# Causal mask of the second row tile's scores: from identity products on TensorE to an add inside VectorE's row maximum

## The reference, cut to what matters

```python
scores = jnp.einsum('bhqd,bhkd->bhqk', q, k) / HEAD_DIM ** 0.5
causal = jnp.tril(jnp.ones((s, s), dtype=bool))
scores = jnp.where(causal[None, None], scores, -jnp.inf)
probs = jax.nn.softmax(scores, axis=-1)
out = jnp.einsum('bhqk,bhkd->bhqd', probs, v)
```

## Time and profile before

| | us |
|---|---|
| median of 3 runs (2930.70 to 2936.34) | 2931.71 |
| profiled execution, its own time | 2930.81 |
| span of that execution in the trace | 2929.1 |
| attention, steady part, 212.31 to 599.00 | 386.69 |

### The profile page before, as it was taken

How to read it: one execution, slowest core, us unless ns; L and a number is a source line. 1 busy time by engine, 2 the same in 40 slices (tenths; PEclk the granted TensorE clock), 3 DMA queues, 4 the chain that set the end, 5 groups by cost and what they waited for, 6 DMA issues and landing times.

```text
span 2929.1 us, 45881 instructions
## 1 busy us (share of the span) xinstructions
PE 2793.4 (95%) x16150; PEld 2283.9 (78%) x16150; DVE 1236.7 (42%) x2152; ACT 877.9 (30%) x1697; POOL 838.8 (29%) x1306
## 2 busy tenths in 40 slices
PE   6989999988999939999999999999999999999998
PEld 6865555556666529999999999999999999999997
DVE  6756777747888833332232232132133133133111
ACT  1126666641555512221121121122122122122110
POOL 4546776631166641101101111011021021011010
PEclk9999999999999969999999999999999999999999
DMA  3101222242122223221122032032033033022010
GB/s 109 43 1 31 48 45 48 55 92 87 68 84 75 77 83 106 91 86 64 51 92 75 26 108 83 15 109 87 12 108 101 11 100 104 14 90 85 26 47 21
DMA packets 97078, 194.68 MB, mean 66 GB/s; under 512 B 22126, under 2 KB 23758, under 8 KB 96800
## 3 DMA queue, kind: packets, MB, share of 16 engines
q1 hardware_dynamic: 75072, 131.77, 15.1%
q0 software_dynamic: 21856, 60.73, 6.6%
HBM read 148.77 MB, written 38.94 MB: 64 GB/s over the span
## 4 chain that ended last, share of the span: by engine, by line
PE 62%; DMA 0%; POOL 0%; DVE 0%; issue 0%; ACT 0%; DVEq 0%; POOLq 0%
PE ex_hid L1775 31%; PE ex_acc L102 10%; PE ex_acc L103 10%; PE ex_acc L104 10%; PE ex_xb L1745 1%; DMA ex_ys<-xn_dram,ex_slot_gather 0%; POOL out_dram L1627 0%; POOL ex_ys L1607 0%; DVE ex_ys L1688 0%; POOL ex_xg L1592 0%; DMA ex_ys<-slot_table_dram 0%; PE ex_acc L1745 0%; DVE ex_h0l L1696 0%; ACT ex_h0h L1655 0%; DVE ex_xT0l L1671 0%
## 5 line engine op out<-in xcount | busy, mean ns | idle before, releaser
L1696 DVE SCALAR_TENSOR_TENSOR ex_h0l<-ex_hid,ex_h0h 128x640 fp32r<-128x640 f32 x128 | 105.5, 824 | 682.8 <-ACT ex_h0h L1655 682.8
L1696 DVE SCALAR_TENSOR_TENSOR ex_h1l<-ex_hid,ex_h1h 128x640 fp32r<-128x640 f32 x128 | 105.4, 824 | 602.9 <-ACT ex_h1h L1655 602.3
L1655 ACT ACTIVATE ex_h0h<-ex_hid 128x640 fp32r<-128x640 f32 x128 | 90.1, 704 | 734.5 <-PE ex_hid L1775 734.5
L1655 ACT ACTIVATE ex_h1h<-ex_hid 128x640 fp32r<-128x640 f32 x128 | 90.1, 704 | 729.8 <-PE ex_hid L1775 729.8
L654 DVE TENSOR_REDUCE at_nb<-at_ring 128x2 f32<-128x512 f32 (+1 forms) x384 | 246.8, 685 | 121.1 <-PE at_ring L760 120.9
L1597 POOL COPY ex_gi<-ex_slot_gather 128x1 int32 (+1 forms) x82 | 15.3, 187 | 918.2 <-PE ex_xb L1745 913.3
L102 PE MATMUL ex_acc<-ex_w_h,ex_h1h 128*128 128x512 f32 x640 | 254.8, 398 | 0.0
L102 PE MATMUL ex_acc<-ex_w_h,ex_h0h 128*128 128x512 f32 x640 | 253.4, 396 | 0.0
L103 PE MATMUL ex_acc<-ex_w_l,ex_h0h 128*128 128x512 f32 x640 | 250.3, 391 | 0.0
L103 PE MATMUL ex_acc<-ex_w_l,ex_h1h 128*128 128x512 f32 x640 | 250.2, 391 | 0.0
L104 PE MATMUL ex_acc<-ex_w_h,ex_h1l 128*128 128x512 f32 x640 | 249.8, 390 | 0.0
(11 more groups left out here) (273 smaller groups left out, 5665.2 us busy)
## 6 DMA issues: line engine op xcount, KB each, us to landing
ex_raw<-in_w_tiles_dram SPq DMA_DIRECT2D x256, 256.0 KB, 2.8
x_in<-in_x_dram SPq DMA_DIRECT2D x32, 256.0 KB, 2.7
act<-at_raw SPq DMA_DIRECT2D x128, 64.0 KB
at_recb<-o_rec_dram SPq DMA_DIRECT2D x16, 512.0 KB
k<-in_x_dram SPq DMA_DIRECT2D x32, 256.0 KB, 2.7
cx_ctx<-in_ctx_dram SPq DMA_DIRECT2D x16, 512.0 KB, 3.8
out_dram<-cx_res SPq DMA_DIRECT2D x16, 512.0 KB, 2.8
xn_dram<-cx_prob SPq DMA_DIRECT2D x16, 512.0 KB, 2.8
```

The source lines that it names most:

```text
L1655: act.activation(h[f % 2][0][:], hid[:, :, 0:HB], ACT.Relu).then_inc(sm["h_hi"], 1)
L1696: dve.scalar_tensor_tensor(h[f % 2][1][:], hid[:, :, 0:HB], 0.0, f32(h[f % 2][0][:]), ALU.max, ALU.subtract).then_inc(sm["h_lo"], 1)
```

## The change

For p = 2 to 5 the mask products on PE are gone. The last score product of each bank now counts `scores`. DVE does for each bank, instead of one `TENSOR_REDUCE` over two heads, one `tensor_tensor_reduce` for each head: it adds the mask to 256 columns, multiplies by -1, writes the result back into the bank and folds it with `min`, starting from 3e38, into one column of `nb`. So the result is again the negated maximum. `mask` is now 256 columns wide (in bfloat16, in SBUF): 128 of zero, then the triangle. The wait for `scores` in front of a masked bank has become an instruction of its own (`wait_apart`). For p = 0 and 1 nothing changes but the slice of `mask`.

```diff
@@ stage_constants
-            pool.affine_select(out=t["mask"][:], in_=t["mask"][:], compare_op=ALU.is_ge, fill=MASKED, base=0,
+            pool.affine_select(out=t["mask"][:, P:S], in_=t["mask"][:, P:S], compare_op=ALU.is_ge, fill=MASKED, base=0,
                                pattern=[[-1, P]], channel_multiplier=1)
@@ stage_attention, dve, step
                             n = 2 * p + r
-                            heads, qb = (slice(0, REP), 0) if p < 2 else (slice(p // 2 * 2 - 2, p // 2 * 2), 1)
-                            dve.wait_ge(sm["scores"], ONE + PIECES * h + n + 1)
-                            dve.tensor_reduce(nb[e][:, r, p % 2, heads, qb],
-                                              bank(e, f"s{n}")[:].rearrange("p (h k) -> p h k", h=heads.stop - heads.start),
-                                              AX.X, ALU.max, negate=True).then_inc(sm["maxima"], 1)
+                            x = bank(e, f"s{n}")
+                            if p < 2:
+                                dve.wait_ge(sm["scores"], ONE + PIECES * h + n + 1)
+                                dve.tensor_reduce(nb[e][:, r, p % 2, :, 0], x[:].rearrange("p (h k) -> p h k", h=REP),
+                                                  AX.X, ALU.max, negate=True).then_inc(sm["maxima"], 1)
+                                continue
+                            wait_apart(dve, sm["scores"], PIECES * h + n + 1, passed_dve)
+                            width, qb, heads = S, 1, range(p // 2 * 2 - 2, p // 2 * 2)
+                            for c, a in enumerate(heads):
+                                y = x[:, c * width:c * width + width]
+                                m = dve.tensor_tensor_reduce(y, y,
+                                                             t["mask"][:, S - width:S], -1.0, LARGEST, ALU.add, ALU.min,
+                                                             nb[e][:, r, p % 2, a, qb:qb + 1])
+                            m.then_inc(sm["maxima"], 1)
@@ stage_attention, pe, score
-                        pe.matmul(banks[r][:, c, :], qs[i][rows, p % 2, n, width - P:width],
-                                  ks[i][rows, p % 2, 0:width], start=True, stop=False, skip_group_check=True)
-                for r in range(2):
-                    pe.matmul(banks[r][:, :, width - P:width], t["identb"][:],
-                              t["mask"][:].unsqueeze(1).to_broadcast([P, len(heads), P]), start=False, stop=True,
-                              skip_group_check=True).then_inc(sm["scores"], 1)
+                        m = pe.matmul(banks[r][:, c, :], qs[i][rows, p % 2, n, width - P:width],
+                                      ks[i][rows, p % 2, 0:width], start=True, stop=p >= 2, skip_group_check=True)
+                        if p >= 2 and c == len(heads) - 1:
+                            m.then_inc(sm["scores"], 1)
+                if p < 2:
+                    for r in range(2):
+                        pe.matmul(banks[r][:], t["identb"][:], t["mask"][:, P:S].unsqueeze(1).to_broadcast([P, REP, P]),
+                                  start=False, stop=True, skip_group_check=True).then_inc(sm["scores"], 1)
@@ decoder_layer
-        t["mask"] = s.sb("mask", [P, P], BF16)
+        t["mask"] = s.sb("mask", [P, S], BF16)
```

More of the change, by code:

```diff
@@ L38 @@
 MASKED = -1e30
+LARGEST = 3e38
 ONE = 1
```

## The result

| | before | after |
|---|---|---|
| median of 19 runs each, us | 2933.25 (2927.45 to 2937.50) | 2938.86 (2936.95 to 2942.94) |
| ratio, 95% interval | | 1.0022 (1.0014 to 1.0029) |
| span of the profiled execution, us | 2929.1 | 2936.9 |
| PE busy in that span, us | 2793.4 | 2778.5 |
| DVE busy in that span, us | 1236.7 | 1278.1 |

The kernel is 0.2% slower. The forecast was 2938.0 us, in a range from 2920 to 2982. PE's records are 14.9 us shorter and DVE's 41.4 longer. The 14.9 is small beside the 82.74 us of the earlier trace rows (which hold the masks of p = 0 and 1 too): records of matmuls overlap, and they are longer where the clock is low.

A forecast was written before the change was run, and what follows sets the result against it. PE and DVE were both taken to lie on the path, handing banks to each other. + 0.095 us a half, 2.9 over 30 halves, plus 3 for the first two made + 6: 2938 us, range 2920 to 2982.

The forecast's parts named there:

- A: Stretch of a half from the shifted scores of p=2 to the scores of p=3: 2.33 us before, forecast 2.66.
- C: Stretch of a half from the scores of p=3 to those of p=5: 4.08 us before, forecast 4.09.
- E: Stretch from the scores of p=5 to the next half's first reduction: 3.01 us before, forecast 2.73, or 2.80 with reciprocal.
- T: Time on DVE from one piece's start to the next, queue full: 0.598 us before, forecast 0.835 (0.81 to 0.856).
- the reads are free: Lower bound for a DVE piece: accumulator reads cost nothing, so start to start is 0.66 us; time 2910.
- second branch: Alternative between the scores of p=3 and p=5: the third piece waits for its scores; 4.02 us, losing to 4.09.
- the one place: From the scores of p=5 to the next half: only there PE's gain was said to arrive, 0.28 us shorter.
- wrong in the method: Failure sign: pieces take 0.83 us and the period still moves by over 0.3 us, so something else came late.
- Rival 1: PE's gain arrives through cheaper DVE pieces: at 0.75 us a piece, - 0.35 a half, 2922 us; chance 0.12.
- The first halves: First two halves of the stage: DVE's added 1.9 us less well covered, put at 1.5 each, 3 us.
- rivals 2 and 3: DVE reads wait for their operation, 2979 us, chance 0.14; no overlap between operations, 3019 us, chance 0.08.
- Rival 4: Added DVE and removed PE work cancel, pieces 0.775 to 0.835 us: 2925 to 2937; chance of same 0.30.

The follow-up runs named there:

- The splits: Against the changed kernel, DVE masks only p=3 and 5, PE p=2 and 4: 2918.93 us; and the mirror, DVE only p=2 and 4: 2959.59 us.
- the two halves of the change: Against the changed kernel: PE's mask products gone with DVE's plain reductions kept, 2900.94 us; DVE's masked pieces with PE's mask products kept too, 2973.97 us.
- the added reduction: Changed kernel plus a DVE reduction of 64 columns behind each masked piece: 2949.52 us, ratio 1.0063.
- the kernel with the old ends: Changed kernel, but the first six and last six halves mask and reduce as before the change: 2933.10 us, ratio 1.0004.
- PE's part alone: Against the changed kernel, plain DVE reductions restored, PE's mask products for p=2 to 5 still gone, second row tile's maxima unmasked: 2900.94 us, ratio 0.9903.
- the split with old ends: Against the changed kernel, DVE masks only p=3 and 5, in the loop's twenty halves; first and last six halves as before the change: 2919.08 us, ratio 0.9955.

## Why the prediction came out right, and where it was wrong

The time, the side and the lengths of A and C were right, and so was that both engines lie on the path in the middle. The sum, + 6 us, was right by luck: of its two terms one had the wrong sign, the other was too small, and a third, the largest, was missing. Of the signs that the prediction named for being right, two came (A at 2.61, E at 2.68) and two did not: pieces are 0.77 apart, not 0.81 to 0.86, and the copies in the middle 12.82, not 12.9 to 13.0.

**The piece** (T = 0.835) is a term that was mis-sized: measured 0.77. An operation with its read was put at 0.41 to 0.43 and takes 0.38. The read's share ("With 0.085 to 0.09 for it") was taken from rows of ACT, where a read delays the next activation by 0.09, and from two short operations 0.09 apart. Here its record starts together with the next operation, and a memset behind each piece lengthened nothing either. If the read is free, as the lower bound "the reads are free, T = 0.66" has it, the operation itself costs 0.38 and not 0.33; the rows don't exclude that a part of the 0.38 is the read.

**The two estimates by the Trainium skill.** By the rule of the Trainium skill, "VectorE: DVE Perf Modes", section "The DRAIN you can't avoid", taken without the exception for operations that are not held, which the same section names, T would have been 1.18; the new operations disagree with that as the reductions did: the next one starts 0.38 us behind one of 0.47. The estimate from the Trainium skill's "Vector Engine (DVE) Microarchitecture Reference", section 5.2, was T = 0.84 and is 0.07 above the measured 0.77: an operation and its read make 0.42 by it, where 0.38 was measured.

**The stretches.** With two pieces at 1.53 (4 x 0.383) the prediction's own formulas give A = 0.99 + 1.53 = 2.52 and C = 2.23 + 1.53 + 0.12 = 3.88 by its second branch. Measured are 2.61 and 4.06, 0.09 and 0.18 more. The terms that were too small are the hand-overs between the engines. In A the first piece starts 0.92 after the shifted scores, where 0.87 stood, and PE starts 0.19 after the next possible start on DVE (351.87 to 352.06), where 0.12 stood. In C the second branch decided, not the one that the prediction named: DVE was free at 354.24 and the third piece started at 354.42, when its scores were there. That is 2.36 after 352.06, where 2.23 stood (that branch had left out the 0.11 of the new wait, though DVE stood idle there), and PE's start comes 1.70 later (356.12), where 2T + 0.12 gives 1.65. E came out at 2.68 for a forecast of 2.73, and the 2.80 for the halves with a reciprocal came in none: PE's gain arrives there, as said. It is not "the one place", though. The splits show it in C as well, - 0.32 through p = 3, which + 0.29 through p = 4 nearly cancels.

Cheaper pieces and dearer hand-overs largely cancelled in A and in C, so that the stretches were met to 0.05 us although T was not. Summed, a half gives - 0.08 where + 0.095 stood, and the middle of the stage - 2.3 where + 2.9 stood. The criterion for "wrong in the method" (pieces at 0.83, period moved by over 0.3) was not met.

**Rival 1**, the faster case, had its point at T = 0.75 with - 0.35 a half, 2922 us. T came out near that point and just below its bound of 0.775, and the half gained only 0.08: the formulas with the measured T give - 0.26 for the three stretches, the hand-overs took 0.27 of it back, and E gave 0.08 more than forecast. So the side of the forecast was not owed to T. It was owed to the hand-overs and to the ends.

**The first halves** ("1.5 each, 3 us") were undersized. It was 3.69 up to the second copy and 5.53 up to the third. The prediction counted only DVE's length there and not that PE would be at its lower clock until 223 us, which makes at least 1.15 of it by the bound above.

**The end of the stage** had no term at all, and it is the largest: 7.0 us from the 31st copy to the output projection, of which the stages behind win back 2.5 (why, no run was made for). The low clock begins at 599 instead of 612 us and lasts 37 us instead of 14, and the windows above show that this is what the time goes into. The prediction read the clock only for the steady part, 1.00, and took it as given; the windows at the two edges of the stage, which show 0.84 and 0.66 before the change, were not read.

The rivals 2 and 3 (T of 1.02 and 1.18) fell with the first rows of L663. Rival 4's condition on T, 0.775 to 0.835, was not met either, though its time nearly was: the measured ratio lies at the bound of 0.2%.

What is shown: that both engines lie on the path in the middle, each at its own places (the two halves of the change, the two splits, the added reduction); that the loss is at the ends (the kernel with the old ends); that a low clock lengthens a half by 2.5 us or more (PE's part alone, third half); that the loss at the end of the stage is the clock (four windows with the same work). What is not: how the loss of the first two halves divides between clock and DVE, and why the clock falls where it does. For the latter the rows give no simple rule: with the same last six halves it fell at about 612 and 609 us in the two profiles of before, at about 607 in the changed kernel with old ends, and at about 588 in the one profile of the split with old ends.

## What to carry to other kernels

Where two engines hand banks to each other, price a moved operation for each place, not each operation: here the same move is worth + 0.28 or - 0.32 us by its phase, and only half of the change should have been made (2918.9 us, the same computation). Before moving work, ask whether it is needed: the maximum serves only to keep the exponential in range, and without any mask on it for the second row tile the kernel takes 2900.9 us, with the reservation that a row's maximum may then be one that the row doesn't see. And look at the granted clock in the windows at the edges of a stage, before and after: in all kernels here whose first halves differ from those of before, whether work was taken from TensorE or DVE's pieces were made longer, the low clock lay over more of them, and that is a cost which no count of instructions shows.

## What the runs showed of the hardware that was not expected

- The accumulator read of DVE has a record of 0.14 us that starts together with the next operation; operation and read together take 0.38 us from start to start. A memset of one column starts 0.08 us into an operation of 0.46. It left the period of the half at 12.82. A reduction of 64 columns, however, takes 0.13 us from start to start.
- The new operation on 256 columns, in place in PSUM with a second operand in bfloat16 from SBUF, takes 0.43 to 0.47 us, and with its read 0.38 from start to start (0.35 behind the first one after a gap).
- TensorE may stay at 1.2 GHz for some 30 us while its records fill nearly all of the time: 18.70 us busy of 20 at a granted clock of 0.50 (190 to 210 us after the change), 17.11 of 20 at 0.84 before. The records are longer at the low clock, so a high busy share there says little of how much PE has to do. From the last copy of maxima to the output projection the same work takes 26.95 us at 0.50, 23.14 at 0.70 and 21.69 at 0.77.
